# Router logits as 32 extra columns of expert 0's gate product, in a perceiver layer with a mixture of experts

## The reference, cut to what matters

```python
x = hidden_states.reshape(-1, H)                 # 256 tokens x 512, normalised
logits = x @ router_w                            # 512 x 32
scores = sigmoid(logits)
# groups of 4 experts: best 4 of 8 groups by the sum of their two best scores,
# then the best 8 experts in them, weights = 2.5 * score / sum of the chosen scores
gate, up = x @ w_gate[e], x @ w_up[e]            # 512 x 256 each
routed  += weight[:, e] * ((silu(gate) * up) @ w_down[e])
shared   = silu(x @ sw_gate) * (x @ sw_up) @ sw_down
```

## Time and profile before

| | us |
|---|---|
| median of 3 runs | 532.94 |
| lowest and highest | 532.65, 533.58 |
| the profiled execution, its own time | 533.22 |
| its span, first to last instruction | 531.2 |

### The profile page before, as it was taken

The page is one execution under the profiler, slowest core; times in us unless marked ns, Lnnn a source line. Parts: engine busy times, 40 slices in busy tenths (PEclk is TensorE's granted clock), DMA queues, the critical chain, the costliest instruction groups (busy, mean ns, idle before and its releaser), DMA issues.

```text
span 531.2 us, 9658 instructions
## 1 busy us (share of the span) xinstructions
PE 521.0 (98%) x3454; PEld 469.3 (88%) x3454; DVE 389.4 (73%) x616; ACT 304.4 (57%) x470; POOL 29.4 (6%) x48
## 2 busy tenths in 40 slices
PE   9999999999989999989999999999999999999997
PEld 7988888888679989879989999999999999999997
DVE  6777555557888987876896777767677777768675
ACT  5655586754376776646646465555646465554631
POOL 1000000000632132010000000000000000000000
PEclk9999999999999999999999999999999999999999
DMA  8765534544412232516355546464554546455521
GB/s 284 289 220 180 201 113 145 166 163 147 136 35 78 85 137 90 192 48 235 122 171 184 191 165 213 150 227 159 199 183 172 203 158 223 146 218 165 190 71 39
DMA packets 19459, 86.24 MB, mean 162 GB/s; under 512 B 2160, under 2 KB 2416, under 8 KB 19312
## 3 DMA queue, kind: packets, MB, share of 16 engines
q1 hardware_dynamic: 19440, 85.99, 47.1%
HBM read 85.46 MB, written 0.52 MB: 162 GB/s over the span
## 4 chain that ended last, share of the span: by engine, by line
PE 93%; DVE 4%; ACT 2%; issue 1%; POOL 0%; ACTq 0%; DVEq 0%; POOLq 0%
PE bank L935 33%; PE bank L429 17%; PE bank L433 16%; PE bank L432 16%; PE bank L437 2%; PE bank L501 1%; PE bank L438 1%; PE bank L439 1%; PE bank L573 1%; PE bank L715 1%; DVE w_lo L282 1%; PE bank L735 1%; PE bank L696 1%; ACT operands L305 1%; PE bank L455 0%
## 5 line engine op out<-in xcount | busy, mean ns | idle before, releaser
L277 ACT CAST w_hi<-raw 128x768 fp32r<-128x768 f32 (+3 forms) x158 | 158.9, 1040 | 96.2 <-PE bank L935 82.8
L282 DVE TENSOR_TENSOR w_lo<-raw,w_hi 128x1280 fp32r<-128x1280 f32 (+3 forms) x156 | 182.8, 1213 | 13.2 <-ACT w_hi L277 11.1
L429 PE MATMUL bank<-w_hi,operands 128*128 128x512 f32 (+1 forms) x322 | 126.4, 393 | 1.2 <-DVE operands L330 0.9
L433 PE MATMUL bank<-w_hi,operands 128*128 128x512 f32 (+1 forms) x322 | 123.9, 385 | 0.0
L432 PE MATMUL bank<-w_lo,operands 128*128 128x512 f32 (+1 forms) x322 | 123.6, 384 | 0.0
L935 PE MATMUL bank<-xt_hi,w_lo 128*128 128x256 f32 x512 | 108.6, 283 | 0.0
L935 PE MATMUL bank<-xt_hi,w_hi 128*128 128x256 f32 x512 | 108.3, 283 | 0.0
L935 PE MATMUL bank<-xt_lo,w_hi 128*128 128x256 f32 x512 | 108.3, 283 | 0.0
L935 PEld LDWEIGHTS bank<-xt_hi,w_hi 128*128 128x128 f32 x512 | 83.7, 190 | 2.6
L935 PEld LDWEIGHTS bank<-xt_lo,w_hi 128*128 128x128 f32 x512 | 81.7, 190 | 0.0
L935 PEld LDWEIGHTS bank<-xt_hi,w_lo 128*128 128x128 f32 x512 | 81.7, 190 | 0.0
(11 more groups left out here) (182 smaller groups left out, 566.5 us busy)
## 6 DMA issues: line engine op xcount, KB each, us to landing
raw<-w_exp_dram SPq DMA_DIRECT2D x34, 896.0 KB, 4.7
raw<-w_exp_dram SPq DMA_DIRECT2D x34, 640.0 KB, 5.7
raw<-ctx_t_dram SPq DMA_DIRECT2D x16, 512.0 KB, 4.7
raw<-ctx_n_dram SPq DMA_DIRECT2D x16, 512.0 KB, 4.3
raw<-w_mla_dram SPq DMA_DIRECT2D x8, 512.0 KB, 3.6
raw<-w_mla_dram SPq DMA_DIRECT2D x8, 448.0 KB, 4.0
raw<-wq_dram SPq DMA_DIRECT2D x4, 256.0 KB, 5.6
raw<-wk_dram SPq DMA_DIRECT2D x2, 512.0 KB, 7.3
```

The costliest lines, as they stand in the source:

```text
L277: act.copy(w_hi[:, t.slot, at:at + n], raw[:, t.slot, at:at + n]).then_inc(hi_split[k], 1)
L282: eng.tensor_tensor(w_lo[:, t.slot, at:at + n], raw[:, t.slot, at:at + n], w_hi[:, t.slot, at:at + n].bitcast(F32), ALU.subtract) \
L429: ins = pe.matmul(o, a[0], b[0], start=start, stop=False)
L433: return pe.matmul(o, a[1], b[0], start=False, stop=stop)
```

## The change

- **Router.** The router weights stand beside expert 0's gate columns: each chunk of gate is 288 columns (256 and 32) in a tile of its own, `w_first`. Expert 0's part a grows from 1280 to 1408 columns (`FIRST_SIZES`), slots grow alike. `first_gate` makes 12 products of 288 columns for each half of the tokens, into banks 4 and 6; `first_up` makes the 12 of up, into banks 2 and 3. The 12 router products, the two transposes of the scores, and the rounding of the router weights at the start are gone. ACT copies 2 x 32 columns of logits out of the banks and takes the sigmoid on rows, 128 x 64.
- **Order.** `transpose_last(1)` goes ahead of an output product; the transposes of half 0 go between the two heads of the last output product; DVE takes the tokens' lo part ahead of the residual's second half; `transpose_hidden(0)` goes into the middle of expert 1's second half; `transpose_hidden(1)` behind `down(0, 0)`.

```diff
-OFF = (0, 1280, 2304)
-SLOT = 3072
+OFF = (0, 1408, 2432)
+SLOT = 3200
+FIRST_SIZES = (1408, 1024, 768)
...
-            for s in range(2):
-                load(Tile(0, T_E + s), w_exp[s], E_SIZES)
+            load(Tile(0, T_E), w_first, FIRST_SIZES)
+            load(Tile(0, T_E + 1), w_exp[0], E_SIZES)
...
             values_last(0)
+            transpose_last(1)
             out_pair(Tile(0, T_M + PAIRS - 2), halves=(1,), heads=(1,))
-            transpose_last(1)
...
-            out_pair(last, last=True, halves=(1,))
+            out_pair(last, last=True, halves=(1,), heads=(0,))
+            transpose_half(xn, 0, 2, xn_ready, 5)
+            out_pair(last, last=True, halves=(1,), heads=(1,))
...
+            def first_gate(h, split, told=None):
+                t = Tile(0, T_E)
+                n = I + E
+                for c in range(NC):
+                    if h == c == 0:
+                        ready(t, 0)
+                    if c % 2 == 0:
+                        pe.wait_ge(ev_lo, split + c // 2)
+                    ins = product(bank[4 + 2 * h][:, 0:n], (xt_hi[:, c, half(h)], xt_lo[:, c, half(h)]),
+                                  wcols(t, c * n, n), c == 0, c == NC - 1, told if c == 0 else None)
+                ins.then_inc(bank_full[4 + 2 * h], 1)
...
-            transpose_half(xn, 0, 2, xn_ready, 5, told=used[1])
-            expert_rows(0, 0, 4, split=V_LN3)
-            expert_rows(1, 0, 5, midway=lambda: transpose_half(xn, 1, 0, xn_ready, 6))
-            expert_rows(0, 1, 6, split=V_LN3 + 2)
-            expert_rows(1, 1, 7, told=used[2])
-            transpose_hidden(0)
+            first_gate(0, V_LN3, told=used[1])
+            first_up(0)
+            second_rows(0, midway=lambda: transpose_half(xn, 1, 0, xn_ready, 6))
+            first_gate(1, V_LN3 + 2)
+            first_up(1)
+            second_rows(1, told=used[2], midway=lambda: transpose_hidden(0))
...
-            pe.wait_ge(rw_split, 1)
-            for c in range(NC):
-                ins = product(bank[6][0:E, 0:T], (rw_hi[:, c, :], rw_lo[:, c, :]),
-                              (xt_hi[:, c, :], xt_lo[:, c, :]), c == 0, c == NC - 1)
-            ins.then_inc(bank_full[6], 1)
+            pe.wait_ge(logits_copied, 2)
+            down(0, 0, told=used[2])
             transpose_hidden(1)
-            down(0, 0, told=used[2])
-            pe.wait_ge(ev_lo, V_H + 1)
-            pe.wait_ge(sigmoid_ready, 1)
-            for h in range(2):
-                ins = pe.transpose(bank[7][:, h * E:h * E + E], score_t[:, half(h)], ident[0:E, 0:E])
-            ins.then_inc(bank_full[7], 1)
             gate_up(0, 2, told=used[1])
...
-            act.wait_ge(small_loaded, 16)
-            act.copy(flat(rw_hi[:, :, :]), smalls[:, C_RW:C_RW + NC * E]).then_inc(consts_rounded, 1)
...
-            pair_step(0, PAIRS - 3, E_SIZES)
+            pair_step(0, PAIRS - 3, FIRST_SIZES)
...
             rows_silu(0, 1)
+            for h in range(2):
+                act.copy(logits[:, h * E:h * E + E], bank[4 + 2 * h][:, I:I + E]).then_inc(logits_copied, 1)
             split_hi(act, Tile(0, T_E + 2), 0, E_SIZES)
+            out_hi(act, 2, F23["h_t"], h_hi[:, 0, :], 512)
             rows_silu(1, 1)
-            for s in range(2):
-                out_hi(act, s, F01["h_t"], h_hi[:, s, :], 512)
-                if s == 0:
-                    split_hi(act, Tile(0, T_E + 2), 2, E_SIZES)
-            act.wait_ge(bank_full[6], F6["router"])
-            act.activation(score_t, bank[6][0:E, 0:T], ACT.Sigmoid).then_inc(sigmoid_ready, 1)
+            split_hi(act, Tile(0, T_E + 2), 2, E_SIZES)
+            out_hi(act, 3, F23["h_t"], h_hi[:, 1, :], 512)
+            act.wait_ge(logits_copied, 2)
+            act.activation(score, logits, ACT.Sigmoid).then_inc(sigmoid_ready, 1)
             split_hi(act, Tile(0, T_E + 3), 0, E_SIZES)
...
             normalize(0, 7)
+            tokens_lo(dve, 2, V_LN3, xt_hi, xt_lo, 0)
             add_to_residual(0, F01["y"], 1, 4)
-            tokens_lo(dve, 2, V_LN3, xt_hi, xt_lo, 0)
             norm_stats(1)
             split_lo(dve, Tile(0, T_E + 1), 0, E_SIZES)
...
             rows_hidden(0, 1)
+            out_lo(dve, 2, V_H, h_hi[:, 0, :], h_lo[:, 0, :], 512)
             split_lo(dve, Tile(0, T_E + 2), 0, E_SIZES)
             rows_hidden(1, 1)
-            out_lo(dve, 0, V_H, h_hi[:, 0, :], h_lo[:, 0, :], 512)
             split_lo(dve, Tile(0, T_E + 2), 2, E_SIZES)
-            out_lo(dve, 1, V_H + 1, h_hi[:, 1, :], h_lo[:, 1, :], 512)
...
-            dve.wait_ge(bank_full[7], F7["score"])
-            dve.tensor_copy(score, bank[7][:, 0:2 * E]).then_inc(score_taken, 1)
```

More of the change, by code:

```diff
@@ L81 @@
 F67 = dict(pv=1, c=2, rows=11)
-F6 = dict(v=3, router=12, moe=13)
-F7 = dict(qk=3, score=12, moe=13)
+F6 = dict(v=3, moe=12)
+F7 = dict(qk=3, moe=12)
 V_LN1, V_Q, V_K, V_V, V_PT, V_OT, V_LN2, V_C, V_M0 = 1, 5, 7, 9, 11, 29, 33, 37, 41
@@ L212, in perceiver_layer @@
         h_row = scores[:, 1, 1024:2048].rearrange("p (r n) -> p r n", r=2)
-        score_t = scores[0:E, 1, 3200:3200 + T]
         def route(at, n):
             return scores[:, 1, 2048 + at:2048 + at + n]
+        logits, score = route(1152, 2 * E), route(0, 2 * E)
         x_loaded = [sem(f"x_loaded{h}") for h in range(2)]
@@ L889, in _, with first_up, second_rows @@
             pe.wait_ge(ev_lo, n + 3)
-            out_pair(last, last=True, halves=(1,))
-            def expert_rows(s, h, b, told=None, split=None, midway=None):
-                t = Tile(0, T_E + s)
+            out_pair(last, last=True, halves=(1,), heads=(0,))
[12 more added lines that the diff above has]
+                ins.then_inc(bank_full[4 + 2 * h], 1)
+            def first_up(h):
+                t = Tile(0, T_E)
+                for c in range(NC):
+                    if h == 0 and c == 1:
+                        ready(t, 2)
+                    at = OFF[2] + (c - 1) * I if c else NC * (I + E)
+                    ins = product(bank[2 + h][:, 0:I], (xt_hi[:, c, half(h)], xt_lo[:, c, half(h)]),
+                                  wcols(t, at, I), c == 0, c == NC - 1)
+                    if h == 1 and c == 0:
+                        ins.then_inc(used[0], 1)
+                ins.then_inc(bank_full[2 + h], 1)
+            def second_rows(h, told=None, midway=None):
+                t = Tile(0, T_E + 1)
                 for u in range(2):
@@ L901, in expert_rows @@
                             ready(t, k)
-                        if split is not None and u == 0 and c % 2 == 0:
-                            pe.wait_ge(ev_lo, split + c // 2)
                         at = (u * NC + c) * I if k == 0 else OFF[2] + (c - 1) * I
-                        ins = product(bank[b][:, u * I:u * I + I], (xt_hi[:, c, half(h)], xt_lo[:, c, half(h)]),
+                        ins = product(bank[5 + 2 * h][:, u * I:u * I + I], (xt_hi[:, c, half(h)], xt_lo[:, c, half(h)]),
                                       wcols(t, at, I), c == 0, c == NC - 1, told if u == c == 0 else None)
@@ L1807 @@
     w_exp = np.concatenate([gate, up[:, :, 0:I], down, up[:, :, I:]], axis=2)
+    router = a["L0_ffn_router_w"].reshape(NC, P, E).transpose(1, 0, 2)
+    first = np.concatenate([gate[0].reshape(P, NC, I), router], axis=2).reshape(P, -1)
+    w_first = np.concatenate([first, w_exp[0, :, NC * I:]], axis=1)
     arrays = {
```

54 lines of the change are left out of this document (25 added, 29 removed).

## The result

| | before | after |
|---|---|---|
| median on the same chip, 5 runs each | 532.80 | 536.44 |
| lowest and highest | 532.59, 533.58 | 535.98, 538.07 |
| the profiled execution | 533.22 | 538.07 |
| its span | 531.2 | 536.2 |
| its mean granted clock | 1.000 | 0.994 |

The change makes the kernel slower, by a ratio of 1.0069 [1.0054, 1.0083], some 3.6 us. The forecast was 1.8 us more, with a range that ended 2.9 us above the median of before. Three of the five runs after have a mean clock of 0.997 (535.98 to 536.44 us) and two have 0.994 (537.97 and 538.07); the profiled one is among the latter.

What follows compares the result with a forecast made beforehand. PE, 98% busy, was taken as bound, except a stretch where an ACT and DVE chain is nearly equally long. Terms 1.5 - 0.1 + 0.45 - 0.1 = 1.75 us on 532.94 gave 534.7 us, range 533.5 to 535.8.

Steps and rivals of the forecast that it cites:

- The chain that it named: From `transpose_hidden(1)` over ACT and DVE to expert 2's lo part: starts 1.5 us later, ends 1.4 later.
- The wait foretold as 3.4 us: PE's wait in front of `down(1, 0)` for expert 2's lo part: grows from 0.3 to about 3.4 us.
- The rival *faster: PE is the bound throughout and its gains come out: 531.3 us; needs the sigmoid before expert 1's eviction; chance 0.08.
- forecast was 0.134: Expert 0's 288-column products: 0.134 us each, bounds 0.12 and 0.24; 24 of them cost 0.3 us more.
- Expert 0 begins at 234.6: Expert 0's first product, after the reordered last output product: at 234.6 instead of 235.44, 0.85 us gained, before the slot's delay.
- The rule of the Trainium skill: Spacing of 131 ns at 512 columns: `down(0, 0)` would take 1.6 us, chain later by 0.1, 533.5 us; not adopted.
- The sigmoid on rows: Sigmoid on 128 x 64 instead of 32 x 256 on ACT: 0.1 us less than 0.37, ends 0 and 0.2.
- part a of expert 0: 128 more columns delay its split and PE: DMA 0.2, ACT 0.12, DVE 0.15, together 0.45 us, ends 0.2 and 0.7.
- The main case: Longer chain and larger part a delay the kernel, everything later shifted by DVE's 1.4: 534.7 us; chance 0.69.
- slower than I have it: Rival: PE idles some 3.4 us before `down(1, 0)`, the clock falls, 2 us lost: 536.7 us; chance 0.07.
- the slot: Expert 0's larger part a, its transfer and splits before the next attention pair's masked scores: 0.45 us later.
- the start: Router weights' rounding leaves ACT and DVE at the kernel's start: 0.1 us gained, at most 0.3 on PE.

Runs made afterwards that it cites:

- The first experiment: Changed kernel with ACT's sigmoid and expert 3's first split ahead of evicting expert 1's hidden tile, DVE's lo part behind its split: 532.55 us, ratio 0.9982.
- seventh: Changed kernel with the first experiment's order, and DVE's lo part of expert 2's hidden tile and next splits ahead of expert 1's additions: 530.98 us, ratio 0.9955.
- eighth: The seventh's kernel with the split of expert 0's larger part a one attention pair later as well: 529.95 us, ratio 0.9937 to the kernel before.
- The tenth experiment: The changed kernel again, unaltered, on another chip: 537.14 us (535.99 to 537.86), ratio 1.0057 to the kernel before.
- The fifth experiment: Kernel before with 120 unused zero columns in expert 0's part a (1400 instead of 1280), nothing else of the change: 533.86 us, ratio 1.0017.
- the third experiment: Changed kernel with 12 products of zeros on PE ahead of `down(1, 0)`, inside its wait: 534.48 us, ratio 1.0017 to the kernel before.
- the fourth experiment: Changed kernel with ACT and DVE splitting expert 0's larger part a one attention pair later: 535.44 us, ratio 1.0031 to the kernel before.
- the second: Changed kernel with DVE's lo part of expert 2's hidden tile ahead of expert 1's two additions: 534.86 us, ratio 1.0020 to the kernel before.

## Why the prediction was right or wrong

**The direction and the mechanism were right.** The chain that it named carries the loss: `transpose_hidden(1)` behind `down(0, 0)`, the eviction of its tile ahead of the sigmoid, and 13 us of DVE work up to the lo part of expert 2's hidden tile. The wait foretold as 3.4 us is 3.33; that the stretch before it came late does not disturb this, since PE and the chain are late alike. The first experiment takes away nothing but ACT's order (and DVE's beside it) and the loss goes. The rival *faster* had named the very condition under which PE's gain would show, the sigmoid ahead of the eviction: the first run, which meets it and nothing else, is 0.2% faster than the kernel before, and the seventh and eighth, with further moves, 0.45% and 0.6%.

**Step by step on PE.** The timeline of the changed kernel, expert 0's gate and the begin of expert 1's:

```profile
235.60 0.37 PE L426 MATMUL bank<-w_hi,xt_hi 128*128 128x288 f32 x1
...
235.93 0.29 PE L430 MATMUL bank<-w_hi,xt_lo 128*128 128x288 f32 x1
...
237.13 0.29 PE L430 MATMUL bank<-w_hi,xt_lo 128*128 128x288 f32 x1
...
238.57 0.28 PE L430 MATMUL bank<-w_hi,xt_lo 128*128 128x256 f32 x1
238.97 0.39 PE L426 MATMUL bank<-w_hi,xt_hi 128*128 128x256 f32 x1
```

From 235.93 to 237.13 nine steps take 1.20 us, 0.133 each; forecast was 0.134, from the 256-column price and the number of columns, and the upper end of 0.24 is out. Expert 0 begins at 234.6 plus 1.0 (forecast plus 0.4), of which 0.92 was there at 212 us. Expert 1's gate is held for 238.97 - (238.57 + 0.12) = 0.28 us (0.3). `down(0, 0)` waits 248.90 - 248.72 = 0.18 (0.15) and takes 2.85 (2.9). The rule of the Trainium skill against which the rows were set ("TensorE: Matmul & The Clock Gate", section "Back-to-back issue gap", 131 ns at 512 columns) does not describe this kernel: its products of 512 start 0.23 apart at full clock, in every profile shown. (By 131 ns the prediction's own terms add up to 533.4 us, not to the 533.5 written.) The sigmoid on rows takes 0.26 instead of 0.37, and the split behind it starts 0.16 after its begin (254.46 - 254.30) instead of 0.28 (252.12 - 251.84): 0.12 saved, as forecast (0.1).

**The term that scatters: part a of expert 0.** The prediction had 0.45 us, of which 0.2 for the transfer. The timelines of ACT and DVE, and the transfer, in the changed kernel's first profile:

```profile
209.91 2.32 ACT L274 CAST w_hi<-raw 128x1408 fp32r<-128x1408 f32 x2 [1.55 <-DMA raw<-w_first_dram]
```

```profile
211.31 1.62 DVE L279 TENSOR_TENSOR w_lo<-raw,w_hi 128x1408 fp32r<-128x1408 f32 x1 [2.06 <-ACT w_hi L274]
212.85 0.48 DVE L1445 CUSTOM_DVE_ANT_0 scores<-bank,smalls,q_neg 128x256 f32<-128x256 f32 x1
```

```profile
raw<-w_first_dram SPq DMA_DIRECT2D x1, 704.0 KB, 5.1
```

ACT starts 0.69 later than before, DVE 0.79, the masked scores 0.92; 0.14 of each was there at 205 us already. So the transfer costs 0.55, ACT 0.10 and DVE 0.13: ACT and DVE as forecast (0.12 and 0.15), the transfer nearly three times its 0.2 and above the end of 0.45 that I had given it. But it is not a fixed price. The same 704 KB land after 4.6 to 5.1 us in seven other profiles and this one, 4.7 in the median, and where they landed in 4.6 (the first experiment) the interval from 205 to 225 us grew by 0.32 and not by 0.77. In the tenth experiment, the same kernel unaltered, they landed in 4.7 and the interval grew by 0.38: there the 0.45 was right. The fifth experiment gives 0.9 with a wide interval. The one row of before, 4.5 us, was taken for a fixed number and its scatter, unknown to me, was not in the ends.

**The step that failed: the clock, given 0.07.** The main case had "everything later is as it was, shifted by DVE's 1.4". It was not: the rival *slower than I have it* came true, with its 536.7 us beside a median of 536.44. All twelve executions of the changed kernel have a mean clock of 0.997 or 0.994, against 12 of 77 of the kernel before, and both profiles show the fall at `down(1, 0)`. The prediction saw the idle time of 3.4 us, had the row of a slow start at the pace of 1.2 GHz, and had nearly the size, 2 us, against 2.7 and 1.6 in the two profiles and 2.1 to 2.8 by the third experiment; it failed in the chance. It counted as evidence against it that the longest idle time in the trace was near 1 us (1.2 by the list of waits) with a clock of 1.00, which says nothing of an idle time three times as long. Without the fall the median would be near 536.44 - 1.4 = 535.0 us, inside the range. The rule cited beside it ("TensorE: Matmul & The Clock Gate", section "Part 1: The HAM clock gate", idle time lowers the clock to half) is what the trace shows: 1.00 before 268, 0.50 from 270. The row of the slow start was weaker evidence than it looks, since it gives a granted clock of 1.00 beside its slow pace (0.44 us for a product, 6.1 us for the first 14, rather than the 0.40 read from it). With this case at even odds the range would have reached 537 and held the result.

**The sum again.** In the first profile the chain is 1.5 for the place of `transpose_hidden(1)`, less 0.1, plus 0.92 of the stretch before it, 2.3 us; the clock is 2.7. That is this execution's 5.0. The tenth experiment's profile is of the same kernel, and its start is another. Counted from PE's transposes near 205 us, in the kernel before and in the tenth:

```profile
205.36 0.49 PE L735 MATMUL bank<-first_rows,scores 128*128 128x128 f32 x3
```

```profile
205.01 0.49 PE L732 MATMUL bank<-first_rows,scores 128*128 128x128 f32 x3
```

`down(1, 0)` comes 267.61 - 205.36 = 62.25 us later before and 269.07 - 205.01 = 64.06 in the tenth, 1.81 more. The prediction's 1.4 for the chain and 0.45 for the slot are 1.85. The products of `down(1, 0)` then take 4.44 us instead of 2.87: the clock costs 1.6 there. So the terms of the main case had their size, and the clock is what was missing. By the times it is less sharp: the median of the first five runs, with 1.4 for the clock (the fourth experiment's groups), leaves 3.6 - 1.4 = 2.2 for chain and slot, while the third experiment's ratio says 0.9 (0.3 to 1.4), though in its profile `down(1, 0)` is late by 1.84 on the same count. Profiled executions differ by up to 0.9 us from the kernel before's at 205 us already, before they reach this stretch, and by the times the split between slot, chain and clock is known no better than that. The term "the start", 0.1 gained, is not visible against this scatter. But one small gain is: the time of an execution exceeds its span by 1.7 to 1.9 us in every run of a kernel with the router beside the gate and by 2.0 to 2.1 in every run of one without, about 0.25 us less. The prediction had nothing for the time outside the span; what makes it shorter is not shown.

## What to carry to other kernels

Before an instruction is moved ahead on the engine that is busy 98% of the time, follow the shortest wait in its list back over the other engines: a wait of 0.3 us was the whole of what PE could gain as long as the chain behind it began no earlier, and an order on ACT decided the rest. When a change opens an idle time of TensorE such as the 3.3 us here, price the slow products that can follow it as well, and consider what else could run there. Read a transfer's time from several executions before it goes into a sum to 0.1 us. Work that nobody waits for (here two additions) belongs behind whatever the bound engine waits for.

## What the runs showed of the hardware

In three profiled executions with a wait of 3.3 us the granted clock fell to one half, 2.4 to 3.7 us after PE had stopped; once it fell near 11.5 us behind a wait of 1.8; in the profiles whose wait was 2.0 or 1.0 it did not. Over all runs, the mean clock was 0.997 or less in 12 of 12 executions of the changed kernel, in 9 of 12 of the fourth experiment with the same wait, in 5 of 12 of the second, in 12 of 77 of the kernel before and in none of the 12 of the first. How long the clock stayed at one half, 3.4 or 6.8 us, differs between executions of one kernel, so the runs form groups, 0.8 to 1.9 us apart by their medians. I had not expected that the same program and wait give different times in this way, nor that products of zeros in the gap would buy back 0.4 to 0.5%. And one transfer of 704 KB, issued at the same place of the same program, took 4.6 to 5.1 us from issue to landing, and the time for which its split held PE went with it.
